# A four-layer transformer stack on one core: the third attention's batches run into each other, and each stage loads its first rows first

## The reference

```python
qkv = norm(x) @ Wqkv.T + bqkv                 # 16 heads of 8, rotary on q and k
scores[g] = sum_h Wpre[g, h] * (q[h] @ k[h].T) / sqrt(8)
probs[g] = softmax(scores[g])                 # [512, 512] for each g
out[h] = (sum_g Wpost[h, g] * probs[g]) @ v[h]
s = concat(out) @ Wout.T + bout               # per batch: [512, 128]
```

## Time and profile before

| engine | busy us | share |
|---|---|---|
| TensorE (PE) | 6193.2 | 89% |
| VectorE (DVE) | 4600.5 | 66% |
| ScalarE (ACT) | 4052.1 | 58% |
| GpSimd (POOL) | 2740.8 | 39% |

### The profile page before, as it was taken

One profiled execution on the slowest core, in us unless ns is written; L12 is line 12 of the kernel. 1 busy time (PEld: TensorE's weight loads), 2 busy tenths in 40 slices (PEclk: granted clock), 3 DMA queues, 4 the chain that ended last, 5 costly groups with the idle time before them and its releaser, 6 DMA issues. The chain is left out here.

```text
span 6967.0 us, 119311 instructions
## 1 busy us (share of the span) xinstructions
PE 6193.2 (89%) x36637; PEld 3361.7 (48%) x36637; DVE 4600.5 (66%) x10942; ACT 4052.1 (58%) x8329; POOL 2740.8 (39%) x2606
## 2 busy tenths in 40 slices
PE   8999997998999789999999979999999999987744
PEld 3444444664222256666666634444444444455544
DVE  4555554665666577777777757777777777776624
ACT  2444443444666567677766757777777777754412
POOL 1222221001677576666666623222222232143345
PEclk9999998999999899999999999999999999999967
DMA  0000001111000111111111100000000000021314
GB/s 10 11 7 10 11 6 36 30 30 31 13 11 12 34 31 32 28 33 31 43 37 43 40 22 3 6 3 3 6 3 6 3 3 6 2 70 58 106 58 118
DMA packets 285664, 182.77 MB, mean 26 GB/s; under 512 B 21124, under 2 KB 266542, under 8 KB 284718
## 3 DMA queue, kind: packets, MB, share of 16 engines
q1 hardware_dynamic: 279964, 163.82, 8.6%
q0 software_dynamic: 4096, 8.40, 0.4%
q10 hardware_dynamic: 1170, 4.85, 0.2%
HBM read 95.81 MB, written 51.38 MB: 21 GB/s over the span
## 5 line engine op out<-in xcount | busy, mean ns | idle before, releaser
L464 PE MATMUL a_scores_ps<-a_kT,a_q_mixed 128*128 128x512 f32 x2048 | 1063.7, 602 | 33.7 <-DVE a_kT L346 30.5
L474 PE MATMUL a_acc_ps<-a_probsT,a_v_post 128*128 128x512 f32 x2048 | 1056.8, 599 | 0.4 <-DVE a_probsT L367 0.4
L276 ACT ACTIVATE a_probs<-a_scores_ps,a_neg_max 128x512 f32<-128x512 f32 x1024 | 703.1, 687 | 555.3 <-DVE a_neg_max L357 546.0
L357 DVE TENSOR_REDUCE a_neg_max<-a_scores_ps 128x1 f32<-128x512 f32 x1024 | 693.0, 677 | 281.3 <-PE a_scores_ps L464 257.3
L367 DVE STREAM_TRANSPOSE a_probsT<-a_probs 128x512 f32<-128x512 f32 x1024 | 716.7, 700 | 136.3 <-PE a_acc_ps L474 106.6
L281 ACT ACTIVATE a_probs<-a_probs,a_inv_sum 128x512 f32<-128x512 f32 x1024 | 728.6, 712 | 9.4 <-DVE a_inv_sum L362 9.4
L773 DVE TENSOR_REDUCE a_neg_max<-a_pair_ps 128x2 f32<-128x1024 f32 (+3 forms) x512 | 416.6, 824 | 378.1 <-PE a_pair_ps L871 372.7
L716 ACT ACTIVATE a_probsT<-a_pair_ps 128x1024 f32<-128x1024 f32 (+3 forms) x512 | 359.4, 704 | 485.3 <-PE a_pair_ps L884 483.8
L474 PEld LDWEIGHTS a_acc_ps<-a_probsT,a_v_post 128*128 128x128 f32 x2048 | 393.7, 192 | 500.0 <-issue 499.8
L464 PEld LDWEIGHTS a_scores_ps<-a_kT,a_q_mixed 128*128 128x128 f32 x2048 | 386.1, 193 | 499.0 <-issue 447.4
L222 POOL TENSOR_TENSOR a_q_mixed<-a_qT,a_pre 128x512 f32<-128x512 f32 x248 | 257.0, 1068 | 840.8 <-PE a_scores_ps L464 840.8
(11 more groups left out here) (399 smaller groups left out, 13204.4 us busy)
## 6 DMA issues: line engine op xcount, KB each, us to landing
f_v_even<-f_v_odd SPq DMA_DIRECT2D x224, 130.0 KB, 2.3
attention_out<-a_s_out SPq DMA_DIRECT2D x64, 256.0 KB, 2.3
f_gs<-attention_out SPq DMA_DIRECT2D x64, 256.0 KB, 3.3
x_after<-f_gout SPq DMA_DIRECT2D x48, 256.0 KB, 2.3
a_x<-x_after SPq DMA_DIRECT2D x48, 256.0 KB
f_x<-x_after SPq DMA_DIRECT2D x48, 256.0 KB, 5.5
f_gx<-x_after SPq DMA_DIRECT2D x48, 256.0 KB, 3.0
f_x_sorted<-f_zeros SPq DMA_DIRECT2D x18, 256.0 KB, 4.3
```

The source lines that it names most:

```text
L276: act.activation(probs[:, n % NPR, :], scores_ps[n % NS][:], ACT.Exp, bias=neg_max[:, n % NS:n % NS + 1], scale=1.0, accum_out=row_sum[:, ...
L357: dve.tensor_reduce(neg_max[:, n % NS:n % NS + 1], scores_ps[n % NS][:], AX.X, ALU.max, negate=True).then_inc(max_ready, 1)
L464: pe.matmul(scores_ps[n % NS][:], q_mixed[:, g % 2, i].rearrange("f a q -> f (a q)"), kT[:], start=True, stop=True).then_inc(scores_ready, 1)
L474: pe.matmul(acc_ps[:], v_post[:, g, i, :], probsT[:, g % NT, i, :], start=(p == 0), stop=(p == U - 1)).then_inc(products_done, 1)
```

## The change

In the third attention: `kT` and the bank of sums are doubled, and the bank and buffer alternate with the batch (`par`); k's addition is done at step 42; the copy of the sum, the output projection and the bias of batch b - 1 are done at steps 21, 24 and 26 of batch b; steps 62 and 63 are finished by steps 0 and 1 of the next batch; the loop has seven rounds of two batches, with a body before and one behind it. Moments move from step 24 to 22, the normalisation from 29 to 28. The values are projected once (four 128x128 products at step 44, one addition at 46) into `v_rows`, and SyncE spreads them into `v` by 16 transfers. `x_copies` and its copy on ScalarE go.

In every stage but the last: SyncE loads x first, then the identity, waits for x to land, and issues half of the other loads; ScalarE issues the other half after the same wait. In the first attention and in the first three feed-forwards VectorE takes the moments (in the third feed-forward only these, otherwise the normalisation too) before it waits for the weights; in the second feed-forward the large fills of `kT`, `v_even` and `v_odd` are cut to the parts that need them, layer 1's weights are loaded three items later, and biases and w2 come in a few transfers of a padded layout; in the first, the two big weights have their own semaphore, which TensorE waits for ahead of its loop. In the third feed-forward the gate's rows of a batch are loaded one body earlier, right behind the issue of the store before them.

```diff
         cos_part, sin_part = sb("cos_part", [D, T]), sb("sin_part", [D, T])
-        qT, kT = sb("qT", [D, T]), sb("kT", [D, T])
+        qT, kT = sb("qT", [D, T]), sb("kT", [D, 2, T])
         q_mixed = sb("q_mixed", [D, 2, NI, NQ, B32])
-        x_copies = sb("x_copies", [D, NI, NQ, B32])
+        v_rows = sb("v_rows", [P, NC, D])
         v = sb("v", [P, NI, D])
...
         scores_ps = [ps(f"scores{n}") for n in range(NS)]
-        acc_ps = ps("acc")
-        p_ps = [ps("p0"), ps("p1"), ps("p2")]
+        acc_ps = [ps("acc0"), ps("acc1")]
+        p_ps = [ps("p0"), ps("p1")]
...
-        MOMENTS, NORMALISE, TURN = 24, 29, 32
+        KEEP_O, FINISH, KEEP_Y = 21, 24, 26
+        MOMENTS, NORMALISE, TURN = 22, 28, 32
         PROJECT_Q, ROTATE_Q, PROJECT_K, ROTATE_K, PROJECT_V = 35, 38, 40, 42, 44
+        def bodies(eng, body):
+            body(0, 0, first=True)
+            with eng.Fori(0, (batches - 2) // 2) as i:
+                body(i * 2 + 1, 1)
+                body(i * 2 + 2, 0)
+            body(batches - 1, 1, last=True)
         block = ctx.enter_context(nc.Block())
...
         def _(sp):
-            for dst, src in loads:
-                sp.dma_start(dst, src).then_inc(weights, 16)
             rows.load(sp, 0, 0)
+            sp.dma_start(*loads[0]).then_inc(weights, 16)
+            sp.wait_ge(rows.x_loaded, 16)
+            for dst, src in loads[2::2]:
+                sp.dma_start(dst, src).then_inc(weights, 16)
+            def move_v(b, first=False):
+                sp.wait_ge(v_kept, b + 1)
+                if not first:
+                    sp.sem_inc(move_begun, 1)
+                    sp.wait_ge(v_post_ready, b * NG)
+                for quarter in range(NQ):
+                    src = v_rows[quarter * B32:(quarter + 1) * B32]
+                    for a in range(NQ):
+                        dst = v[a * B32:(a + 1) * B32].rearrange("p (c r) d -> p r c d", r=NQ)[:, quarter]
+                        sp.dma_start(dst, src).then_inc(v_ready, 16)
...
-            with sp.Fori(0, batches - 1) as b:
-                rows.load(sp, b + 1, b + 1)
-                store(b)
+            move_v(0, True)
+            def body(b, par, first=False, last=False):
+                if not last:
+                    rows.load(sp, b + 1, b + 1)
+                if not first:
+                    store(b - 1)
+                if not last:
+                    move_v(b + 1)
+            bodies(sp, body)
             store(batches - 1)
...
                 if g == 0:
-                    pool.wait_ge(v_ready, b * 4 + 4)
+                    pool.wait_ge(v_ready, b * MOVES + MOVES)
                 pool.wait_ge(products_done, b * U + (g + 1 - NG) * NI)
...
         def _(act):
+            act.wait_ge(rows.x_loaded, 16)
+            for dst, src in loads[1::2]:
+                act.dma_start(dst, src).then_inc(weights, 16)
             def exps(b, n, first):
...
-            def copies(b):
+            def keep_xT(b):
                 act.wait_ge(rows.xn_turned, b + 1)
-                act.activation(rows.xT[:], p_ps[2][:], ACT.Copy).then_inc(rows.xT_ready, 1)
-                act.activation(x_copies[:], p_ps[2][:].rearrange("d (i q) -> d i q", i=NI).unsqueeze(2)
-                               .to_broadcast([D, NI, NQ, B32]), ACT.Copy).then_inc(copies_ready, 1)
+                act.activation(rows.xT[:], p_ps[0][:], ACT.Copy).then_inc(rows.xT_ready, 1)
-            def keep_oT(b):
+            def keep_oT(b, par):
                 act.wait_ge(products_done, b * U + U)
-                act.activation(oT[:], acc_ps[:], ACT.Copy).then_inc(oT_ready, 1)
+                act.wait_ge(y_ready, b + 1)
+                act.activation(oT[:], acc_ps[par][:], ACT.Copy).then_inc(oT_ready, 1)
             def step(b, n, first=False):
-                if n < U:
-                    exps(b, n, first)
+                exps(b, n, first)
                 if n >= 1:
                     scale_probs(b, n - 1)
+                elif not first:
+                    scale_probs(b - 1, U - 1)
             act.sem_inc(oT_ready, 1)
-            copies(0)
+            act.sem_inc(y_ready, 1)
+            keep_xT(0)
             for n in range(PV_LAG):
...
-            def rotate_k(b):
+            def rotate_k(b, par):
                 rotate_parts(b, 1)
                 dve.sem_inc(k_parts, 1)
+                dve.tensor_tensor(kT[:, par, :], cos_part[:], sin_part[:], ALU.add).then_inc(k_ready, 1)
-            def finish_k():
-                dve.tensor_tensor(kT[:], cos_part[:], sin_part[:], ALU.add).then_inc(k_ready, 1)
-            def keep_v(b, m):
-                dve.wait_ge(v_projected, b * 4 + (m + 1))
-                dve.tensor_tensor(v[:, 4 * m:4 * m + 4, :], p_ps[m % 3][:].rearrange("p (i d) -> p i d", i=4),
-                                  b_v[:].unsqueeze(1).to_broadcast([P, 4, D]), ALU.add).then_inc(v_ready, 1)
+            def keep_v(b, first=False):
+                dve.wait_ge(v_projected, b + 1)
+                if not first:
+                    dve.wait_ge(v_ready, b * MOVES)
+                dve.tensor_tensor(v_rows[:], p_ps[0][:].rearrange("p (c d) -> p c d", c=NC),
+                                  b_v[:].unsqueeze(1).to_broadcast([P, NC, D]), ALU.add).then_inc(v_kept, 1)
...
             def keep_y(b):
-                dve.wait_ge(y_ready, b + 1)
+                dve.wait_ge(y_ready, b + 2)
                 dve.wait_ge(s_free, b + 1)
-                dve.tensor_tensor(s_out[:], p_ps[2][:].rearrange("p (c d) -> p c d", c=NC),
+                dve.tensor_tensor(s_out[:], p_ps[1][:].rearrange("p (c d) -> p c d", c=NC),
                                   b_out[:].unsqueeze(1).to_broadcast([P, NC, D]), ALU.add).then_inc(s_ready, 1)
...
-            def body(b, last):
+            def body(b, par, first=False, last=False):
                 chain.restart()
-                for n in range(PV_LAG, U + 2):
+                for n in range(PV_LAG, U):
                     step(b, n)
+                    if n == KEEP_Y and not first:
+                        keep_y(b - 1)
                     if not last:
...
                         if n == ROTATE_K:
-                            rotate_k(b + 1)
-                        if n >= PROJECT_V + 2 and n < PROJECT_V + 6:
-                            keep_v(b + 1, n - PROJECT_V - 2)
-                        if n == U - 1:
-                            finish_k()
-                if not last:
+                            rotate_k(b + 1, 1 - par)
+                        if n == PROJECT_V + 2:
+                            keep_v(b + 1)
+                if last:
+                    turn_probs(b, U - 2)
+                    invert(b, U - 1)
+                    turn_probs(b, U - 1)
+                    keep_y(b)
+                else:
                     for n in range(PV_LAG):
                         step(b + 1, n)
-                keep_y(b)
-            with dve.Fori(0, batches - 1) as b:
-                body(b, False)
-            body(batches - 1, True)
+            bodies(dve, body)
...
-            def project_v(b, m):
-                if m == 0:
-                    pe.wait_ge(copies_ready, b + 1)
-                    pe.wait_ge(k_parts, b + 1)
-                if m == 3:
-                    pe.wait_ge(v_ready, b * 4 + 1)
-                for j in range(4):
-                    i = 4 * m + j
-                    last = pe.matmul(p_ps[m % 3][:, j * D:(j + 1) * D], x_copies[:, i].rearrange("d a q -> d (a q)"),
-                                     w_in[:, 2, :], start=True, stop=True)
+            def project_v(b):
+                pe.wait_ge(rows.xT_ready, b + 1)
+                pe.wait_ge(k_parts, b + 1)
+                for c in range(NC):
+                    last = pe.matmul(p_ps[0][:, c * D:(c + 1) * D], rows.xT[:, c * P:(c + 1) * P], w_in[:, 2, :],
+                                     start=True, stop=True)
                 last.then_inc(v_projected, 1)
-            def scores(b, n, first=False):
+            def scores(b, par, n, first=False):
                 g, i = divmod(n, NI)
...
                     pe.wait_ge(v_post_ready, b * NG + (g + 1))
-                if p == 0:
-                    pe.wait_ge(oT_ready, b + 1)
-                pe.matmul(acc_ps[:], v_post[:, g, i, :], probsT[:, g % NT, i, :], start=(p == 0),
+                if p == 0 and not first:
+                    pe.wait_ge(oT_ready, b)
+                pe.matmul(acc_ps[par][:], v_post[:, g, i, :], probsT[:, g % NT, i, :], start=(p == 0),
                           stop=(p == U - 1)).then_inc(products_done, 1)
-            def finish(b, last):
+            def finish(b):
                 pe.wait_ge(oT_ready, b + 2)
-                if not last:
-                    pe.wait_ge(v_ready, b * 4 + 8)
                 for c in range(NC):
-                    last = pe.matmul(p_ps[2][:, c * D:(c + 1) * D], oT[:, c * P:(c + 1) * P], w_out[:],
```

(61 more changed lines are left out.)

677 lines of the change are left out of this document (358 added, 319 removed).

## The result

The changed kernel takes 6772.5 us (median of four runs, 6766.8 to 6782.1), against 6969.6 us before: a ratio of 0.971, 95% interval 0.970 to 0.973. Forecast: 6771 us. The medians differ by 197.1 us. The profiled execution was the fastest of the four; its span is 6765.0 us, 202.0 less than before. The working gave 198.4.

The account below looks back on a forecast made before the run. The prediction took the third attention to be bound by TensorE's stream plus its waits at batch borders. Savings of 161 - 2 + 39.4 = 198.4 us gave 6772 beside the median of 6970.46, stated as 6771; range 6750 to 6812.

Parts of the forecast that it names:

- The batch: Third attention: TensorE's instructions sum to 115.6 us a batch against 126.3 before; 15 x 10.7 = 161 us saved.
- the values: Third attention: three of four groups of value products go from TensorE, 3 x 0.89 = 2.7 us a batch.
- kT: Third attention, batch border: TensorE's wait for the finished keys goes, 2.2 us a batch.
- the clock: Third attention: TensorE no longer drops to its lower level after idle stretches at batch borders, 2.3 us a batch.
- the bank: Third attention, batch border: wait for the copy of oT goes, 3.5 us a batch; 5.8 with the 2.3 of lower clock.
- The returns: Third attention's loop jumps: VectorE stalls about 2.5 us, mostly absorbed; 0.3 us each at the output projection, 2 us lost.
- the first rival: Third attention: VectorE falls over four steps behind, TensorE waits at each loop return and its clock falls; 31 us, 6802; chance 0.13.
- the second: Third attention: TensorE itself stalls 2.5 us at each loop return and its clock falls; 31 us, 6802; chance 0.04.
- The moves: Third attention: sixteen transfers spreading v take 10 us a batch, within 47.7 us of slack; hidden, cost 0.
- The starts: Stage beginnings, plus the third feed-forward's end: x first and loads shared over two queues; 39.4 us saved.
- The terms of the attentions: Attention starts, loads over two queues: third saves 7 us, first and second 3.5 each, fourth loses 1.6.
- The third rival: Stage starts: landing of weights is the bound, two queues share transfer engines; only 10 of 39 us come, 6800; chance 0.08.

Follow-up runs that it names:

- after_again: The changed kernel itself, unaltered, profiled a second time beside other edited kernels on the same chip: 6774.8 us, ratio 0.9723 to the kernel before.

## Why the prediction was right

**The batch.** 115.6 forecast, 115.53 measured; 15 x 10.77 = 161.6 against 161. The sum holds because TensorE is the only bound: all that was left to do was to add up its instructions. The division of the 10.7 among the parts was less good. Undone one by one, the values cost 2.7 (forecast 2.7), kT 4.0 (2.2 and a share of the clock), the bank 7.0 (5.8): 13.7, more than the 10.8 that all bring together. The clock is not a part of its own that belongs to the wait for oT; either of the two waits, left alone, takes it along at nearly every border.

**The returns.** Forecast 2 us lost, measured nothing. The term was small and the reason partly wrong. The prediction put its 0.3 us at the output projection, which is the right place, but it took the margin from the four score banks, and the nearest limit was the copy of the sum. It held by 0.9 us. The gap was 1.5 us and not the 2.5 of the earlier trace rows; why it was shorter, no run shows, and with 2.5 the margin would have been used up. So the first rival (0.13) was missed by less than a microsecond, and that it was missed is in part luck; the second didn't occur.

**The moves.** Hidden, as forecast. They took 11.9 us (12.6 in the batch shown), not 10: an issue took 0.64 us, not 0.48. Slack 36 us at the start.

**The starts.** By first turns: second feed-forward 14.4 (forecast 14), first 7.4 (7), first and second attention 3.6 and 2.8 (7 together), third feed-forward 4.0 at the start and 1.8 at the end, where VectorE's wait is 7.53 now (6), fourth attention -1.5 (-1.6). The third attention has 4.1 at its first turn (5), and 4.0 at its first scores, not 7: the group of products that went saved 1.8, but the second pair of projections ran at the lower clock (3.75 us; 1.96 in the kernel before) and took that back. This was the execution's chance: in `after_again` the pair took 1.95 and the first scores came 6.0 us sooner than before. Sum of the starts: 14.4 + 7.4 + 6.4 + 5.8 + 4.0 - 1.5 = 36.5, against 39.4. With 161.6 that is 198.1 of the 202.0; the other 4 lie in stages that move by as much without an edit. A gain at the first turn isn't always kept to the end of the stage: the third feed-forward is 3.0 us shorter, not 5.8.

That the total came out within 2 us of the median is also a matter of errors that offset each other: 2 us for the returns that weren't lost, and 3 us less at the starts.

The weakest step of the reasoning was the second queue. The terms of the attentions share the weights over two queues, and taking the second away moved the first turns by 1.7 us in six stages together. The third rival had this right (two queues load no faster than one), and still its conclusion, 10 of the 39 us, did not come true. Of what did pay, only the fewer bytes were undone by themselves (some 6 us). That x goes first, that moments and normalisation lie beside the landing, the shorter fills and the earlier load of the gate's rows were not taken back one by one; their shares are read from the first turns, and not shown apart.

## What to carry to other kernels

Where one engine is busy without a gap, the time of a reordered loop can be added up from its instructions, and what is left to check is the margin of everything that follows it, each against its nearest reader. A stall of TensorE of 2.0 us in such a stream cost 4.0, its length and nearly as much in clock; one of 1.65 us cost its length alone; and several stalls don't add. At a start, let each engine wait for its first operand only (15 us here); a second queue for the same bytes brought next to nothing. And before a few microseconds of one stage are explained from two profiles, look at how far that stage moves between profiles of one kernel.

## What the hardware did that I had not expected

An addition of two 128x512 tiles in SBUF took VectorE 0.69 us alone and 1.34 when it met a GpSimd instruction already running: 0.65 of the old wait of 2.04 for kT was this. TensorE had no gap at any return of the loop, with its first instruction right behind the jump, where VectorE had 1.5 to 1.7 (changed kernel) and 2.5 to 2.8 us (before). And the lower clock came behind 14 of 15 waits of about 2 us in one kernel, behind nine of 15 in another, and not behind one of eight of 3.8 us: how long the wait is doesn't settle it.
